# A four-layer graph network: where the complement of the mask bytes is made, and which queue stores it

## The reference, cut to what matters

```
h = jnp.maximum(_layernorm(x, axis=-1), 0.0)
e = jnp.einsum('bid,bjd,dk->bkij', hidden, hidden, A)
e = leaky_relu(e)
scores = where(adj == 1, e[:, 0], -9e15)      # adj holds 0 and 1 only
out = softmax(scores) @ hidden
```

## Time and profile before

| | us |
|---|---|
| median of 3 runs | 1757.23 (1756.17 to 1760.38) |
| profiled execution | 1756.96 |
| its span | 1755.2 |
| PE busy | 1500.6 (85%) |
| DVE busy | 1305.9 (74%) |
| ACT busy | 1200.0 (68%) |
| POOL busy | 177.1 (10%) |
| mean of the granted TensorE clock | 0.953 of full |

### The profile page before, as it was taken

One profiled execution on the slowest core, in us unless ns is written; L12 is line 12 of the kernel. 1 busy time (PEld: TensorE's weight loads), 2 busy tenths in 40 slices (PEclk: granted clock), 3 DMA queues, 4 the chain that ended last, 5 costly groups with the idle time before them and its releaser, 6 DMA issues. The chain is left out here.

```text
span 1755.2 us, 33849 instructions
## 1 busy us (share of the span) xinstructions
PE 1500.6 (85%) x12740; PEld 1198.3 (68%) x12740; DVE 1305.9 (74%) x3853; ACT 1200.0 (68%) x1857; POOL 177.1 (10%) x201
## 2 busy tenths in 40 slices
PE   3999996999259798999989899899999899998963
PEld 3999995555146486876868677686776768667652
DVE  3666654887356787888878888798888878887753
ACT  2778871222455878888888887878878788885741
POOL 3444410000000000000001000010000001000000
PEclk9999996999579899999999999999999999999976
DMA  9999952677112122222221222312212222111011
GB/s 188 207 212 209 219 121 74 240 240 271 52 37 79 42 61 61 55 61 79 72 62 49 67 61 67 85 49 61 61 57 78 72 60 53 51 55 49 8 30 38
DMA packets 108456, 162.03 MB, mean 92 GB/s; under 512 B 9344, under 2 KB 59136, under 8 KB 106240
## 3 DMA queue, kind: packets, MB, share of 16 engines
q1 hardware_dynamic: 85248, 117.86, 22.4%
q0 software_dynamic: 18432, 33.56, 10.4%
q10 hardware_dynamic: 4608, 8.39, 1.4%
HBM read 151.40 MB, written 41.94 MB: 110 GB/s over the span
## 5 line engine op out<-in xcount | busy, mean ns | idle before, releaser
L1277 PE MATMUL ps<-fac_A,mask_A 128*128 128x258 f16 x2048 | 245.4, 274 | 51.6 <-DVE agg L922 37.9
L1277 PE MATMUL ps<-fac_C,mask_C 128*128 128x258 f16 x2048 | 239.0, 275 | 35.3 <-DVE agg L922 21.6
L1277 PEld LDWEIGHTS ps<-fac_A,mask_A 128*128 128x128 fp8e4 x2048 | 195.3, 98 | 99.7 <-DVE agg L922 53.0
L1339 PE MATMUL ps<-hV,wts 128*128 128x129 f32 x2048 | 250.1, 278 | 13.0 <-DVE xC L954 9.9
L1339 PEld LDWEIGHTS ps<-hV,wts 128*128 128x128 f32 x2048 | 240.6, 194 | 17.3 <-DVE xC L954 13.0
L1277 PEld LDWEIGHTS ps<-fac_C,mask_C 128*128 128x128 fp8e4 x2048 | 197.3, 98 | 73.0 <-DVE agg L922 25.3
L942 DVE SCALAR_TENSOR_TENSOR wts<-lk,wts 128x1024 f32<-128x1024 f32 x128 | 154.3, 1217 | 21.9 <-ACT wts L1179 21.9
L1177 ACT ACTIVATE lk<-ps 128x1024 f32<-128x1024 f32 x128 | 131.8, 1030 | 53.2 <-DVE wts L942 30.0
L307 ACT ACTIVATE maskT<-ps 128x1024 fp8e4<-128x1024 bf16 x128 | 131.1, 1024 | 53.0 <-PE ps L341 41.5
L1179 ACT ACTIVATE wts<-ps,shiftB 128x1024 f32<-128x1024 f32 x128 | 143.7, 1123 | 0.0
L1155 ACT ACTIVATE mask_A<-s_row,steep_t_A 128x1024 fp8e4<-128x1024 f32 x128 | 141.1, 1141 | 1.8
(11 more groups left out here) (239 smaller groups left out, 3243.6 us busy)
## 6 DMA issues: line engine op xcount, KB each, us to landing
adj_b<-in_adj POOLq DMA_DIRECT2D x128, 256.0 KB, 9.0
maskT_scratch<-maskT SPq DMA_DIRECT2D x16, 1024.0 KB, 6.9
ring_A<-maskT_scratch SPq DMA_DIRECT2D x64, 256.0 KB, 3.1
off<-maskT_scratch SPq DMA_DIRECT2D x32, 512.0 KB, 4.1
ring_C<-maskT_scratch SPq DMA_DIRECT2D x64, 256.0 KB, 3.2
xa<-in_x SPq DMA_DIRECT2D x16, 512.0 KB, 4.4
whT_scratch<-whT_s ACTq DMA_DIRECT2D x32, 256.0 KB, 6.4
whT_b<-whT_scratch SPq DMA_DIRECT2D x16, 512.0 KB, 4.9
```

The lines of the kernel that those rows point to most:

```text
L1277: last = nc.tensor.matmul(Q_SLOTS[c % 2][:, k, 0:XW], m_fp8[x][:, k, j, c * P:c * P + P], fac[x][:, k, j, :], start=(j == 0), stop=(j == T ...
L1339: last = nc.tensor.matmul(Q_SLOTS[c // 2 % 2][:, c % 2, 0:PW], wts[:, j, c * P:c * P + P], hV[b % 2][:, j, :], start=(j == 0), stop=(j == ...
```

## The change

In the second stage a new ScalarE step `no_edges(b)` makes the complement from `maskT`, in two halves of 4 tiles. It reads the bytes two at a time as 16-bit integers and computes 2056 - value (2056 is 0x0808), which is the complement of both bytes; the constant comes from a small tile `two_edges` that VectorE fills once. The result goes to `off_b` (two halves), and GpSimd's queue stores each half to a new array `offT_dram`. A half is written again only after its store of the graph before has landed. SyncE waits for stores before it loads `off` and at the end of the stage. In the last stage `load_off` reads `offT_dram`, `complement` and its semaphore are gone, and `gram` waits for the load itself.

```diff
+        offT_dram = nc.dram_tensor("offT_scratch", (B, P, T, N), u8).ap()
...
+            off_b = sbb("off_b", [P, 2, T // 2, N], u8)
+            two_edges = sbb("two_edges", [P, 1])
...
+                    for h in range(2):
+                        sp.wait_ge(b_off_out[h], 16)
...
-                        sp.dma_start(off[:, 4 * h:4 * h + 4, :], maskT_dram[0, :, 4 * h:4 * h + 4, :]).then_inc(off_in[h], 16)
+                        sp.dma_start(off[:, 4 * h:4 * h + 4, :], offT_dram[0, :, 4 * h:4 * h + 4, :]).then_inc(off_in[h], 16)
...
+                        sp.wait_ge(b_off_out[par], B * 16)
...
+                    nc.vector.memset(two_edges[:, :], float(EDGE * 257)).then_inc(b_two, 1)
                     graph(0, 0, True)
...
                 def _(pool):
+                    for b in range(B):
+                        for h in range(2):
+                            pool.wait_ge(b_off, 2 * b + h + 1)
+                            pool.dma_start(offT_dram[b, :, h * T // 2:(h + 1) * T // 2, :], off_b[:, h, :, :]).then_inc(b_off_out[h], 16)
...
+                    def no_edges(b):
+                        for h in range(2):
+                            if b > 0:
+                                act.wait_ge(b_off_out[h], b * 16)
+                            nc.scalar.activation(off_b[:, h, :, :].bitcast(u16), maskT[:, b, h * T // 2:(h + 1) * T // 2, :].bitcast(u16),
+                                                 ACT.Identity, bias=two_edges[:, 0:1], scale=-1.0).then_inc(b_off, 1)
+
                     graph(0, 0, 0, True)
                     graph(1, 1, 0, True)
+                    act.wait_ge(b_two, 1)
+                    no_edges(0)
                     people(0, 0, 0, True)
                     graph(2, 0, 1, False)
                     people(1, 1, 0, True)
                     graph(3, 1, 1, False)
+                    no_edges(1)
                     for k in range(1, B // 2 - 1):
                         for par in range(2):
                             people(k * 2 + par, par, k, False)
                             graph(k * 2 + 2 + par, par, k + 1, False)
-                    for par in range(2):
-                        people(B - 2 + par, par, B // 2 - 1, False)
+                            no_edges(k * 2 + par)
+                    no_edges(B - 2)
+                    people(B - 2, 0, B // 2 - 1, False)
+                    no_edges(B - 1)
+                    people(B - 1, 1, B // 2 - 1, False)
...
-                    def complement(b, h):
-                        dve.wait_ge(S["B", "ring"][h], (b + 1) * 16)
-                        nc.vector.tensor_scalar(off_int[:, 4 * h:4 * h + 4, :], off_int[:, 4 * h:4 * h + 4, :], EDGES, None,
-                                                ALU.bitwise_xor).then_inc(S["B", "off"], 1)
...
-                        if AA:
-                            complement(i, 0)
-                            complement(i, 1)
...
                         if j % 4 == 0:
-                            pe.wait_ge(S["B", "off"], 2 * b + j // 4 + 1)
+                            pe.wait_ge(S["B", "ring"][j // 4], (b + 1) * 16)
```

More of the change, by code:

```diff
@@ L11, in gnn_stack_kernel @@
     fp32, i32 = mybir.dt.float32, mybir.dt.int32
-    fp16, bf16, u8 = mybir.dt.float16, mybir.dt.bfloat16, mybir.dt.uint8
+    fp16, bf16, u8, u16 = mybir.dt.float16, mybir.dt.bfloat16, mybir.dt.uint8, mybir.dt.uint16
     fp8 = mybir.dt.float8e4
-    EDGE, EDGE_VALUE, EDGES = 8, 2.0 ** -6, 0x08080808
+    EDGE, EDGE_VALUE = 8, 2.0 ** -6
     ALU = mybir.AluOpType
@@ L536, in gnn_stack_kernel @@
             pT_b = sbb("pT_b", [P, 2, N])
+            off_b = sbb("off_b", [P, 2, T // 2, N], u8)
+            two_edges = sbb("two_edges", [P, 1])
+            b_off, b_off_out = stage_sem("b_off"), [stage_sem(f"b_off_out{k}") for k in range(2)]
+            b_two = stage_sem("b_two")
             b_mask_out = [stage_sem(f"b_mask_out{k}") for k in range(2)]
@@ L714, in gnn_stack_kernel @@
             ring_int = {x: ring[x][:, :, :].bitcast(i32) for x in cases}
-            off_int, off_fp8 = off[:, :, :].bitcast(i32), off[:, :, :].bitcast(fp8)
+            off_fp8 = off[:, :, :].bitcast(fp8)
             LK = 3
@@ L755, in gnn_stack_kernel @@
                 S["C", n] = csem(f"C_{n}")
-            for n in ("var", "rstd", "shift", "h", "hT_made", "ahi", "lo", "off", "gram", "exps", "wts", "tile", "done"):
+            for n in ("var", "rstd", "shift", "h", "hT_made", "ahi", "lo", "gram", "exps", "wts", "tile", "done"):
                 S["B", n] = csem(f"B_{n}")
@@ L792, in load_off @@
                             sp.wait_ge(S["B", "gram"], (b - 1) * T + 4 * h + 4)
-                        sp.dma_start(off[:, 4 * h:4 * h + 4, :], maskT_dram[b, :, 4 * h:4 * h + 4, :]).then_inc(S["B", "ring"][h], 16)
+                        sp.dma_start(off[:, 4 * h:4 * h + 4, :], offT_dram[b, :, 4 * h:4 * h + 4, :]).then_inc(S["B", "ring"][h], 16)
                     def load_q(b):
```

## The result

The changed kernel takes **1799.91 us** (median of 4 runs, 1798.66 to 1802.37) against 1757.72 for the kernel before on the same chip: 1.024 times as long, 95% interval 1.0222 to 1.0258. The forecast was 1795, with a range from 1784 to 1816.

The account below looks back on a forecast made before the run. It took the second stage as set by TensorE's 8.69 us step with a ring 0.1 us short of it, and the last by three interdependent engines: 1756.96 + 54.7 - 16.8 = 1794.9, so 1795 us, range 1784 to 1816.

Parts of the forecast that it names:

- The ring and its slack of 0.1 us: Second stage: people, stats, graph(b+2) and cast take 8.58 us of an 8.69 us step; ScalarE's idle 6.41 us lie inside.
- The instruction: Second stage, ScalarE: one no_edges half takes 2.01 us, counted as 1.90 with overlap, 3.8 us for a pair.
- The rival of faster two-byte elements: Second stage: ScalarE's instructions take 1.04 us each, so the stage loses only 29.2 us; 1769 in all; chance 0.03.
- Eleven steps: Second stage, people(2) to people(13): 11 steps of 12.28 us instead of 8.69, 39.5 us slower.
- `people(13)` to `people(14)`: Second stage's end: two pairs, the second waiting for stores of 5 us; 19.2 us, which is 10.5 more.
- `people(14)` to `people(15)`: Second stage's end: no_edges(15) waits 3.1 us for a store, then 3.8; 6.9 instead of 8.31 us, 1.4 less.
- The last stage: Last stage: without VectorE's complement, TensorE's wait shrinks by 1.20 us 14 times; 16.8 us faster.
- The rival "gives nothing back": Last stage: TensorE's next wait takes the 1.20 us, so nothing is gained; 1812 us; chance 0.08.
- The idle time takes it: Second stage: ScalarE's idle 6.41 us per graph absorb the 3.8 us, only the last stage's gain stays; 1740 us; chance 0.05.
- The stores come late: Second stage: stores over 10.4 us make no_edges wait in every graph; at 12 us, 1827 in all; chance 0.08.
- At nothing: TensorE's clock and the DMA engines: Second stage: slower clock after TensorE's pauses and the added 1 MB of stores per graph were both taken to cost nothing.
- GpSimd's descriptors and VectorE's second port: Second stage's end: clamp L594 blocks GpSimd's descriptor writes, each of two last waits up to 0.69 us longer; 1796, otherwise 1795.

Follow-up runs that it names:

- the fast version: The changed kernel with ScalarE's pair for graph b+2 between people(b) and the cast of graph(b+2), none at the stage's end: 1745.06 us, ratio 0.9931.
- the other order: The changed kernel with ScalarE's pairs two graphs ahead, between people and the cast, and without the 32 stores and their waits: 1738.92 us, ratio 0.9896.

## Why the prediction was right, point by point

- **The ring and its slack of 0.1 us: right.** ScalarE's idle 6.41 us stayed 6.41 in every graph. The same instructions in the idle time gave back the step of 8.69; half as long they gave 1.71 back of 1.71.
- **The instruction: right.** 1.99 us for 2.01, a pair 3.8 us until the next start for 3.8. The rival of faster two-byte elements is out, by the 1.14 us at 1024 elements.
- **Start of the stage: right.** 6.3 us for 6.1.
- **Eleven steps: right.** 39.2 us for 39.5; a step is 12.25 for 12.28.
- **`people(13)` to `people(14)`: the mechanism was right, the size was not.** 15.7 us for 10.5. The mis-sized quantity is the store, taken at 5 us between 2.9 and 9.0 because "this queue has nothing else in it here". It took 9.8. The queue was indeed empty; the DMA engines that serve it were full with SyncE's loads for the last stage and its mask store. I had read their share of 0.72 in the middle of the stage and not at its end, where this one store mattered. The rows on which the bound of 9.0 rested were the better ones for this place.
- **`people(14)` to `people(15)`: right in kind.** 3.1 us less for 1.4 less. The store that this wait hangs on was issued at 490.46, by then with free DMA engines, and landed in 2.9 us; I had used 5 here as well.
- **The last stage: right, a little small.** 17.9 us for 16.8; alone 16.4. The wait ahead of tile 2 is 0.43 us, the number that the forecast had left. The rival "gives nothing back" is out.
- **The other rivals.** "The idle time takes it" is out by the step of 12.25. "The stores come late" needed over 10.4 us in every graph: the median of the 32 is 2.9 and the longest 9.8. It came near at the one place where SyncE's loads stand ahead.
- **The forecast's own range does not follow from its terms.** 1787 to 1808 was given for the longer instruction and the store of 9 us. The two together give 1811, and stores of 2.9 give 1791. The result lies inside either way.
- **At nothing: TensorE's clock and the DMA engines.** The granted clock was 0.90 of 2.4 GHz in the window from 402 to 419, so a part of it ran at the lower level of 1.2. TensorE was busy for 13.85 of these 17 us and had waited up to 2.9 us at a time for the clamp; before, at 17.00 of 17.00, the clock was 1.00. The step stayed at 12.25. Over whole steps, from one `people` to the next, the DMA share was 0.69 to 0.72, no higher than before (the windows of 17 us shown above hold uneven parts of the steps). Both held, save at the stage's end.
- **GpSimd's descriptors and VectorE's second port, priced at 0.69 us a wait.** In the changed kernel the case does not arise: in a step GpSimd's issues start at 343.55 and 345.44 and the clamp at 339.52, each 12.25 us later in the next. The two at the end that ScalarE waits for start at 478.30 and 490.46, with no clamp beside them. All took 0.53 us but one, 0.60. With the pair in the idle time it does arise (GpSimd's and VectorE's timelines there):

```profile
354.76 0.53 POOL L640 DMA_DIRECT2D offT_scratch<-off_b  x1 [7.18 <-ACT off_b L665]
356.65 0.78 POOL L640 DMA_DIRECT2D offT_scratch<-off_b  x1 [1.36 <-ACT off_b L665]
```

```profile
356.61 0.69 DVE L603 TENSOR_SCALAR row<-row 128x1024 f32<-128x1024 f32 x1
```

The issue that starts with the clamp takes 0.78 us instead of 0.53 and ends at 357.43, 0.13 behind the clamp; the next one, at 365.23 with a clamp from 365.31 on, takes 0.88 and ends 0.11 behind it. By the rule of the Trainium skill, "SBUF — State Buffer", section "SBUF: two separate sides", GpSimd cannot write descriptors until such a VectorE operation ends: the trace of this version agrees, at 0.25 and 0.35 us, the rest of a short clamp. In the fast version one issue took 1.01 us (from 332.90, clamp from 333.10) and again ended 0.12 behind the clamp. No such delay moved the step.

By engine time alone, the reading that the forecast gave beside the Trainium skill, "ScalarE: Activation LUTs", section "Rules for kernel authors", the move would have cost 42.6 us. The total, 42.2 us between the medians, happens to be that number, and the reading is still wrong: in the other order the same instructions cost nothing (1738.92, without their stores, against 1740.99 without them). A right total does not prove a reading; here two readings gave nearly the same total, and only moving the pair told them apart.

The sum: 1.2 + 6.3 + 39.2 + 15.7 - 3.1 - 17.9 = 41.4 us of span. The forecast was 54.7 - 16.8 = 37.9. The 3.5 between are 5.2 of the late store, 1.7 (to `people(15)`) and 1.1 (last stage) the other way, and 1.2 ahead of the second stage, where nothing was forecast; the other terms are off by 0.1 together. That the total is off by only 3.5 is in part luck: the late store and the two smaller misses have opposite signs.

## What to carry to other kernels

An engine's idle time is yours only if it lies outside the loop that sets the pace: follow one unit of work through all in-order engines, add up the ring, and compare it with the step before adding anything. Then put the new work where the engine already waits, ahead of the instruction that it waits for there and as far ahead of its user as its input allows, so that none is left for the end of the stage (here this was worth 8 us, 1753 against 1745). A store or a load must be priced at the place where someone waits for it, with what the other queues have just sent to the same DMA engines, and a wait must be checked on every in-order queue that it is put on: moved to SyncE, the same stores cost 4 us or 84 by their place alone.

## What the runs showed of the hardware that was not expected

- In the fast version the DMA engines of the core were busy for 0.97 of the window shown and moved 358 GB/s, and for 0.95 to 1.00 of every window of 17 us from 317 to 419, and TensorE was busy throughout. A 512 KB store then landed in 6.2 us in the median instead of 2.9.
- The first cast of the second stage stands behind the same first stage in all kernels here, and came between 296.6 and 304.0 us in the profiled executions. Some versions have a little work just ahead of it (a fill of a small tile in most, a fill of `off_b`, or one pair on ScalarE), but the latest comes from a version with the small fill alone, like the changed kernel with 298.06. With one trace of each kernel the cause stays open. A difference of a few microseconds has to be read from points inside one stage, or from medians.
